# Two macaron layers with routed experts on one core: own slots for every block, and three smaller edits

## The chip, the cores and the metric

One core of a Trainium2 chip runs the kernel. TensorE (PE in the profile) multiplies matrices into PSUM, VectorE (DVE) and ScalarE (ACT) work elementwise and read PSUM, GpSimd (POOL) issues the indirect transfers, and SyncE (SP) issues all others. The time is that of the whole program on the device, in microseconds (us). Every engine runs its own list of instructions in order; they wait for each other only through semaphores.

## The reference, cut to what matters

There are 2048 tokens of width 128. A layer is: half a routed feed-forward, attention, half a routed feed-forward. There are two such layers, so four feed-forward stages (s = 0 to 3), with attention after stage 0 (squared-relu attention over 256 tokens) and after stage 2 (linear attention with a running sum).

```
x = x + 0.5 * L0_ffn(layernorm(x))     # stage 0
x = x + L0_attn(layernorm(x))
x = x + 0.5 * L0_ffn(layernorm(x))     # stage 1
x = x + 0.5 * L1_ffn(layernorm(x))     # stage 2
x = x + L1_attn(layernorm(x))
x = x + 0.5 * L1_ffn(layernorm(x))     # stage 3

# a feed-forward: rms norm, scores = xn @ router.T, the best 2 of 8 experts,
# h = u * silu(gate), y = h @ w_down[e].T, the two y weighted and summed, plus the skip
# linear attention: kv = cumsum_t(K_t outer V_t); out_t = Q_t . kv_t / (Q_t . cumsum(K)_t)
```

## The kernel before

**Tiles and parts.** The tokens form 4 blocks (b0 to b3) of 512. In each stage a block's 1024 (token, expert) pairs are sorted by expert into 15 tiles of 128 rows, each with one expert. The 16 parts (stage s, block b) follow each other: 240 tiles in all, one tile per *slot* t. PE in slot t multiplies tile t with the up and gate weights (`up`, L1045 for layer 0 with 256 hidden units, L1052 for layer 1 with 352), and then tile t-2 with the down weights (`down`, L1006 and L1008), for which DVE must have made u * silu(gate) of that tile (`mult`, L698), which in turn waits for ACT's silu (L593). PE can thus run some two slots ahead of DVE and no further; three PSUM banks hold the up and gate results.

**Rows.** Every four tiles (a round) SP loads 512 sorted rows (L395), PE transposes them into bank S[2] (`rows`, L1067), and ACT copies them (L598). The load of a round stands five slots ahead of its tiles in SP's list, and it waits until all eight scatters of its block have landed; the weights of a tile (L409) stand four slots ahead, in the same list, and so behind such a wait. Round 0 of the first part isn't loaded: DVE makes 0/1 matrices (`onehot`, L871 and L874) and PE sorts the rows by multiplying with them (L1061).

**The side chains.** Beside the tiles each block goes through: gather its y rows from DRAM (POOL, eight indirect transfers, L525), `combine` (DVE, L745), attention after stages 0 and 2 (steps 3 to 21), and `route` for the next stage: `stats` (L702), `guess` (variance and an inverse root of ten dependent small steps, L708 to L726), `norm` (L730), `skip` (L783, and ACT's L610), `z` (PE transposes, L1078), `score` (PE L1083, DVE L793), `first` and `second` (the two best experts), `rank` (PE L1089), `assign` (DVE, L844 to L862, the row numbers), `weights`, and `scatter` (POOL, eight indirect transfers, L504). Where a step stands is read from tables: `ROUTE`, `ATTENTION` and `COMBINE` give the slot of each step, counted from `end_of(s, b)`, which is where the block's part ends (for the first routing it is `LEAD` slots ahead of the block's first part). `WAY` says which row of the tables a block uses; before, nearly all blocks use row 0. Slots ahead of 0 hold no tiles: there the tables set only the order of the steps. A step's slot is a place in every engine's list, not a time; on POOL there is nothing else in the list, so a later slot there means later only where another POOL step comes in between.

**Bank S[2].** `z`, `score`, `rank` and `rows` take turns in it (`S2_TURN`). PE's `claim` waits until all earlier turns have been read: `rows` after a `score` waits for DVE's L793, after a `rank` for DVE's L850. In PE's list a slot goes: up, down, rows, and then the chains' steps, in order of the block's chain.

**POOL in the second attention.** Steps 13 to 16 form the outer products of K and V (L559) on POOL; ACT rounds them (L651) and DVE forms the rest (L895), for the running sums on PE (L1167, L1168).

## Time and profile before

| | |
|---|---|
| runs | 741.56, 747.86, 764.09 us (median 747.86) |
| profiled execution | 741.62 us, span 739.9 us |
| PE busy | 620.9 us (84%), 4590 matmuls |
| DVE busy | 456.0 us (62%) |
| ACT, POOL busy | 264.9 us (36%), 281.8 us (38%) |
| mean granted PE clock | 0.941 of full speed |
| chain that ended last | PE 50%, DVE 26%, issue 9%, DMA 6% |

A share is of the whole span, over stages with different limits. The parts are between 32 and 54 us long: the first matmul of the first tile starts at 34.6 us; parts of stage 0 without and with attention beside them, the parts of stage 1, and so on differ in what runs beside the tiles. Idle time of an engine costs only where it lies on the chain.

### The profile page before, as it was taken

Reading aid. Unit: us, or ns where it says so; the run is one execution under the profiler, and the core shown is the slowest. Engines: PE = TensorE matmul, PEld = TensorE weight load, DVE = VectorE, ACT = ScalarE, POOL = GpSimd, SP = SyncE. Lnnn points to the kernel's source line nnn. Section 1 sums busy time; section 2 is a strip of 40 time slices with the busy share of each in tenths; the row PEclk is TensorE's granted clock in tenths of the full one; section 3 lists DMA queues with packets and bytes.
Section 4 is the critical chain, followed back from the end, with each engine's and each line's share of the span. In section 5 each row is a group of like instructions: output and inputs, shape, how many; then the busy total and the mean of one; then the engine's idle time right before and its main releaser. Section 6 shows DMA issues by size and latency. Waiting matters only on the chain.

```text
span 739.9 us, 15773 instructions
## 1 busy us (share of the span) xinstructions
PE 620.9 (84%) x4590; PEld 567.5 (77%) x4590; DVE 456.0 (62%) x1649; ACT 264.9 (36%) x549; POOL 281.8 (38%) x327
## 2 busy tenths in 40 slices
PE   1688798987969888778888987989979979988977
PEld 1377778777768787777877987978868968877966
DVE  7765545827448257455445664967967969763445
ACT  2134342532514324333323344326326326323221
POOL 2444552160440613563514446044245147052314
PEclk9999999999998999989899999979969989999989
DMA  7388786645545457757656885645645645657752
GB/s 257 102 242 277 220 248 181 181 125 163 163 126 157 125 166 207 229 171 231 204 155 192 246 246 162 170 135 153 189 137 142 196 123 163 203 156 230 236 138 74
DMA packets 113271, 133.59 MB, mean 181 GB/s; under 512 B 10931, under 2 KB 76227, under 8 KB 112806
## 3 DMA queue, kind: packets, MB, share of 16 engines
q1 hardware_dynamic: 104998, 115.79, 53.9%
q0 software_dynamic: 8192, 16.79, 7.6%
q8 instruction: 42, 0.69, 0.4%
q14 instruction: 39, 0.32, 0.1%
HBM read 103.83 MB, written 28.71 MB: 179 GB/s over the span
## 4 chain that ended last, share of the span: by engine, by line
PE 50%; DVE 26%; issue 9%; DMA 6%; another core or an unknown queue 3%; ACT 3%; POOL 2%; POOLq 0%; DVEq 0%; SPq 0%
PE up_gate L1052 13%; PE up_gate L1045 10%; PE y L1006 8%; DVE hidden L698 4%; DVE x_res L745 3%; DMA rows_dram<-rms_out,rows_of 2%; PE side L1067 2%; PE y L1008 2%; PE side L1133 2%; DMA y_rows<-y_dram,rows_of 2%; PE side L1149 2%; PE side L1083 1%; DVE root_square L725 1%; DVE root_square L724 1%
## 5 line engine op out<-in xcount | busy, mean ns | idle before, releaser
L698 DVE TENSOR_TENSOR hidden<-up_gate,hidden 128x256 f32<-128x256 f32 (+1 forms) x240 | 115.5, 489 | 193.7 <-ACT hidden L593 79.1
L504 POOL DMA_INDIRECT rows_dram<-rms_out,rows_of x128 | 129.8, 1014 | 249.7 <-DVE rows_of L855 183.2
L1052 PE MATMUL up_gate<-rows_T,up 128*128 128x128 f32 x1440 | 196.6, 287 | 21.0 <-ACT rows_T L598 8.7
L1052 PEld LDWEIGHTS up_gate<-rows_T,up 128*128 128x128 f32 x1440 | 182.1, 200 | 30.0 <-issue 15.6
L525 POOL DMA_INDIRECT y_rows<-y_dram,rows_of x120 | 121.0, 1008 | 183.5 <-issue 119.3
L593 ACT ACTIVATE hidden<-up_gate 128x256 f32<-128x256 f32 (+1 forms) x240 | 103.9, 436 | 240.8 <-PE up_gate L1045 112.8
L1045 PE MATMUL up_gate<-rows_T,up 128*128 128x128 f32 x960 | 139.5, 291 | 13.4 <-issue 9.0
L1045 PEld LDWEIGHTS up_gate<-rows_T,up 128*128 128x128 f32 x960 | 126.4, 203 | 24.1 <-issue 22.1
L1006 PE MATMUL y<-down,hidden 128*128 x480 | 77.9, 287 | 16.7 <-DVE hidden L698 14.8
L1006 PEld LDWEIGHTS y<-down,hidden 128*128 128x128 f32 x480 | 67.1, 202 | 18.4 <-issue 18.4
L1006 PE MATMUL y<-down_a,hidden 128*128 x480 | 75.9, 282 | 0.0
L598 ACT ACTIVATE rows_T<-side,norm 128x512 f32<-128x512 f32 x64 | 42.3, 661 | 81.0 <-PE side L1067 41.2
L1006 PEld LDWEIGHTS y<-down_a,hidden 128*128 128x128 f32 x480 | 65.9, 199 | 0.0
L586 ACT ACTIVATE y_tile<-y 128x512 f32<-128x512 f32 x64 | 36.5, 570 | 48.9 <-PE y L1008 25.0
L1008 PE MATMUL y<-down_b,hidden 96*128 x240 | 48.0, 282 | 0.0
L1067 PE MATMUL side<-ident,rows 128*128 128x128 f32 x236 | 37.9, 282 | 8.0 <-DVE row_of L850 4.4
L1008 PEld LDWEIGHTS y<-down_b,hidden 96*128 96x128 f32 x240 | 37.9, 198 | 0.1
L1078 PE MATMUL side<-ident,rms_out 128*128 128x128 f32 x64 | 12.4, 326 | 29.4 <-DVE rms_out L730 22.6
L1067 PEld LDWEIGHTS side<-ident,rows 128*128 128x128 f32 x236 | 28.8, 146 | 9.3 <-issue 8.6
L1078 PEld LDWEIGHTS side<-ident,rms_out 128*128 128x128 f32 x64 | 8.5, 165 | 31.0 <-issue 16.2
L610 ACT ACTIVATE x_res<-x_res,b_skip_add,b_skip_mul 128x128 f32<-128x128 f32 x64 | 26.2, 482 | 8.7 <-issue 4.9
L745 DVE SCALAR_TENSOR_TENSOR x_res<-y_rows,w_first,x_res 128x128 f32<-128x128 f32 x64 | 24.1, 418 | 5.4 <-DMA y_rows<-y_early,early_rows_of 3.7
(195 smaller groups left out, 698.3 us busy)
## 6 DMA issues: line engine op xcount, KB each, us to landing
up<-in_up SPq DMA_DIRECT2D x120, 352.0 KB
up<-in_up SPq DMA_DIRECT2D x120, 256.0 KB
rows<-rows_dram SPq DMA_DIRECT2D x47, 256.0 KB
y_dram<-y_tile SPq DMA_DIRECT2D x45, 256.0 KB
rows_dram<-zeros SPq DMA_DIRECT2D x12, 256.0 KB, 3.3
rows<-rows_dram SPq DMA_DIRECT2D x16, 192.0 KB
y_dram<-y_tile SPq DMA_DIRECT2D x15, 192.0 KB
rows_dram<-rms_out,rows_of POOLq DMA_INDIRECT x128
```

The costliest lines, as they stand in the source:

```text
L504: pool.indirect_dma_start(out=xg_d[g], out_offset=bass.IndirectOffsetOnAxis(ap=pos[g][:, at:at + 1], axis=0), in_=xs(Z, GROUPS[g][c // TB] ...
L525: pool.indirect_dma_start(out=gath[b % 2][:, (TB * k2 + c) * P:(TB * k2 + c + 1) * P], out_offset=None, in_=y_d[g], in_offset=bass.Indirec ...
L586: act.activation(ysb[r % 4][:, 0:n * P], Y[r % 2][:, 0:n * P], ACT.Copy).then_inc(y_done, 1)
L593: act.activation(hid[n % 4][:, 0:w], src, ACT.Silu).then_inc(silu_done, 1)
L598: act.activation(xgT[r % 3][:, 0:n * P], S[2][:, 0:n * P], ACT.Copy, scale=wn[:, LAYER[s]:LAYER[s] + 1]).then_inc(s2_free, 1)
L698: dve.tensor_tensor(h, u, h, ALU.mult).then_inc(mult_done, 1)
L745: last = dve.scalar_tensor_tensor(xs(X, b, c * P, P), gath[b % 2][:, (TB * k2 + c) * P:(TB * k2 + c + 1) * P], wk[:, c:c + 1], xs(X, b, c ...
L1006: last = pe.matmul(y, hid[n % 4][:, c * P:(c + 1) * P], w, start=(c == 0), stop=(l == 0 and c == 1))
L1008: last = pe.matmul(y, hid[n % 4][0:96, 2 * P:3 * P], dn1b[:, bass.ds(v * P, P)], start=False, stop=True)
L1045: last = pe.matmul(U[q % 3][:, i * P:(i + 1) * P], upW[n % RING][:, at:at + P], rows_, start=True, stop=True)
L1052: last = pe.matmul(U[q % 3][:, c * P:(c + 1) * P], upW[n % RING][:, at + c * P:at + (c + 1) * P], rows_, start=True, stop=True)
L1067: last = pe.transpose(S[2][:, c * P:(c + 1) * P], xg[r % 4][:, c * P:(c + 1) * P], ident[:, :])
```

## The change

Four edits. (1) Each block gets its own row of the tables (`WAY` becomes 0, 1, 2, 3 in every stage), and nearly all slots move; `LEAD` goes from 38 to 40; `guess` gets a wait for the last block's `skip_ready`, as `skip` may now stand behind it. (2) The outer products of the second attention go from POOL to DVE, at the same steps 13 to 16. (3) The row numbers 1 to 512 (two memsets and a scan) are made at the head of DVE's list, not in the first `score`. (4) `onehot` finishes its matrices one after the other and releases each; PE waits for each. Of the tables only the entries are shown that matter here (both stand for slots after `end_of`):

```diff
-LEAD = 38
+LEAD = 40
 COMBINE, stages 0, 1, 2, 3
-  ((8, 10),), ((11, 16),), ((7, 13),), ((7, 10),)
+  ((7, 8) x4), ((10, 15) x4), ((8, 11), (6, 8), (6, 11), (6, 11)), ((10, 11), (9, 9), (9, 10), (9, 10))
 ATTENTION[0], block 0
-  3: 11, 4: 11, 5: 12, 6: 12, 7: 14, 8: 15, 9: 16, 10: 17, 11: 18, 12: 19, 13: 19, 14: 20, 15: 21
+  3: 8, 4: 11, 5: 11, 6: 12, 7: 15, 8: 16, 9: 16, 10: 16, 11: 17, 12: 17, 13: 18, 14: 18, 15: 19
+  (block 1: steps 12 to 15 all at 18; block 2: 10 to 14 all at 17, 15 at 18)
 ATTENTION[2], blocks 0 and 1
-  3: 13, 4: 14, 5: 15, 6: 16, 7: 17, ... 13: 22, 14: 22, 15: 23, 16: 24, ... 20: 29, 21: 30
+  3: 11, 4: 14, 5: 15, 6: 15, 7: 17, ... 13: 21, 14: 23, 15: 24, 16: 25, ... 20: 29, 21: 30
+  3: 13, 4: 14, 5: 15, 6: 15, 7: 17, ... 13: 21, 14: 21, 15: 24, 16: 25, ... 20: 29, 21: 30
 ROUTE[0], blocks 0, 1, 2, 3 (before: rows 1, 2, 0, 0)
-  b0 stats 8, guess 10, root 11, norm 16, skip 17, z 20, score 23, first 23, second 23, rank 24, assign 24, weights 27, scatter 30
-  b1 stats 5, guess 7, root 8, norm 8, skip 13, z 13, score 18, first 18, second 18, rank 23, assign 23, weights 26, scatter 24
-  b2, b3 stats 3, guess 3, root 8, norm 8, skip 15, z 9, score 12, first 12, second 15, rank 17, assign 17, weights 25, scatter 23
+  b0 stats 4, guess 15, norm 18, skip 18, z 19, score 20, first 23, second 24, rank 24, assign 27, weights 33, scatter 41
+  b1 stats 3, guess 8, norm 9, skip 17, z 10, score 15, first 17, second 18, rank 25, assign 25, weights 29, scatter 33
+  b2 stats 1, guess 5, norm 7, skip 18, z 8, score 10, first 16, second 16, rank 16, assign 17, weights 25, scatter 32
+  b3 stats 1, guess 5, norm 7, skip 18, z 8, score 10, first 15, second 15, rank 15, assign 16, weights 24, scatter 31
 ROUTE[1]
-  stats 21, guess 21, norm 23, skip 31, z 26, score 27, first 28, second 28, rank 30, assign 30, weights 30, scatter 30
+  stats 19, guess 20, norm 21, skip 28, z 23, score 24, first 24, second 27, rank 29, assign 29, weights 33, scatter 29
 ROUTE[2]
-  stats 16, guess 17, norm 20, skip 31, z 22, score 23, first 24, second 25, rank 27, assign 27, weights 36, scatter 29
+  stats 15, guess 16, norm 18, skip 23, z 19, score 20, first 22, second 24, rank 26, assign 26, weights 38, scatter 29
 ROUTE[3]
-  stats 30, guess 30, norm 30, skip 37, z 32, score 32, first 32, second 32, rank 34, assign 34, weights 35, scatter 37
+  stats 31, guess 31, norm 31, skip 41, z 33, score 34, first 34, second 34, rank 35, assign 35, weights 37, scatter 41
-WAY = ((1, 2, 0, 0), (0, 0, 0, 0), ...)
+WAY = ((0, 1, 2, 3), (0, 1, 2, 3), ...)
```

```diff
 # guess
+                    after(dve, skip_ready, k - 1)
 # first score
-                        dve.memset(R[5], 1.0)
-                        link(dve.memset(R[4], 1.0))
-                        link(dve.tensor_tensor_scan(R[4], R[5], R[4], 0.0, ALU.mult, ALU.add))
 # onehot
-                    last = dve.tensor_scalar(R[c], R[4], rows_1[:, 2 * c:2 * c + 1], None, ALU.is_equal)
-                link(last)
-                for c in range(TB):
-                    last = dve.scalar_tensor_tensor(R[c], R[4], rows_1[:, 2 * c + 1:2 * c + 2], R[c], ALU.is_equal, ALU.add)
-                last.then_inc(onehot_ready, 1)
+                    link(dve.tensor_scalar(R[c], R[4], rows_1[:, 2 * c:2 * c + 1], None, ALU.is_equal))
+                    dve.scalar_tensor_tensor(R[c], R[4], rows_1[:, 2 * c + 1:2 * c + 2], R[c], ALU.is_equal, ALU.add).then_inc(onehot_ready, 1)
 # attention, taken out of POOL's list and put into DVE's
+                if l == 1 and j in (13, 14, 15, 16):
+                    ...
+                    dve.tensor_tensor(R[3 + t].rearrange("p (h f g) -> p h f g", f=F, g=G),
+                                      kk.unsqueeze(3).to_broadcast([P, HEADS, F, G]),
+                                      vv.unsqueeze(2).to_broadcast([P, HEADS, F, G]), ALU.mult).then_inc(kv_ready, 1)
 # ahead of DVE's first slot
+            dve.memset(R[5], 1.0)
+            link(dve.memset(R[4], 1.0))
+            link(dve.tensor_tensor_scan(R[4], R[5], R[4], 0.0, ALU.mult, ALU.add))
 # PE, rows of round 0
-                    pe.wait_ge(onehot_ready, 1)
                     claim("rows", r)
                     for c in range(TB):
+                        pe.wait_ge(onehot_ready, c + 1)
                         last = pe.matmul(S[2][:, :], xs(Z, 0, c * P, P), R[c], start=(c == 0), stop=(c == TB - 1))
```

## Rows read from the trace of the kernel before

**Rows 1.** Busy time by stretch: us, then each engine's busy us, PE clock, DMA share.

```profile
99.00:139.70 40.70, 37.54 (x268) 32.98 (x268) 22.58 (x90) 16.05 (x33) 10.11 (x11) 1.00 0.72 209
139.70:186.90 47.20, 41.34 (x274) 36.37 (x274) 26.13 (x110) 17.77 (x38) 15.93 (x16) 0.93 0.51 148
...
478.60:533.00 54.40, 49.27 (x346) 44.28 (x345) 43.40 (x129) 21.51 (x42) 20.96 (x20) 0.87 0.54 156
...
587.30:640.00 52.70, 46.47 (x346) 42.59 (x346) 44.60 (x134) 21.29 (x42) 21.40 (x20) 0.94 0.57 165
```

**Rows 2.** Timeline of the start: start us, us long, engine, line, what, [idle before <-releaser].

```profile
9.77 0.38 DVE L708 BATCH_NORM_AGGREGATE b_meanvar<-b_stats 128x2 f32<-128x6 f32 x4
...
12.59 0.17 DVE L726 SCALAR_TENSOR_TENSOR b_rstd<-root_square,b_rstd 128x8 f32<-128x8 f32 x1
...
15.25 0.19 DVE L793 COPY scores<-side 128x32 f32<-128x32 f32 x1
...
26.57 0.18 DVE L793 COPY scores<-side 128x32 f32<-128x32 f32 x1
...
26.90 5.96 PE L1061 MATMUL side<-attention,rms_out 128*128 128x512 f32 x8 [2.83 <-DVE attention L874]
...
34.55 1.15 PE L1045 MATMUL up_gate<-rows_T,up 128*128 128x128 f32 x8 [1.69 <-issue]
```

**Rows 3.** Timeline: the third block's first transposes, and the first scatters' end.

```profile
31.86 0.97 POOL L504 DMA_INDIRECT rows_dram<-rms_out,rows_of  x1 [0.30 <-issue]
...
34.17 0.38 SPq L395 DMA_DIRECT2D rows<-rows_dram  x1
...
40.19 0.66 PE L1078 MATMUL side<-ident,rms_out 128*128 128x128 f32 x4 [3.38 <-DVE rms_out L730]
```

**Rows 4.** Timeline of POOL: first and last gather of b0, last gather of b1.

```profile
76.05 1.04 POOL L525 DMA_INDIRECT y_rows<-y_dram,rows_of  x1 [4.00 <-DMA rows_dram<-rms_out,rows_of]
...
86.57 0.99 POOL L525 DMA_INDIRECT y_rows<-y_dram,rows_of  x1 [0.33 <-issue]
...
120.17 1.00 POOL L525 DMA_INDIRECT y_rows<-y_dram,rows_of  x1 [0.30 <-issue]
```

**Rows 5.** Timeline of PE: the first transposes of the third and fourth parts' rows.

```profile
94.61 0.60 PE L1067 MATMUL side<-ident,rows 128*128 128x128 f32 x4
...
136.85 0.63 PE L1067 MATMUL side<-ident,rows 128*128 128x128 f32 x4 [1.10 <-DVE scores L793]
```

**Rows 6.** Chain of waits, 660 to 690 us: start us, us, what was waited for.

```profile
673.78 5.27 DMA rows_dram<-rms_out,rows_of
...
679.10 3.03 DMA rows<-rows_dram
```

**Rows 7.** Timeline: a down matmul beside the stage-1 routing.

```profile
173.38 0.71 PE L1006 MATMUL y<-down,hidden 128*128 x4 [2.70 <-DVE hidden L698]
```

**Rows 8.** Timeline at the last routing of the second block.

```profile
539.11 0.87 DVE L702 BATCH_NORM_STATS2 b_stats<-x_res 128x6 f32<-128x128 f32 x4
...
544.22 1.11 PE L1078 MATMUL side<-ident,rms_out 128*128 128x128 f32 x4 [2.97 <-DVE rms_out L730]
```

**Rows 9.** Busy time in stretches of 2 us, columns as in rows 1.

```profile
544.00:546.00 2.00, 1.11 (x4) 0.71 (x4) 2.00 (x7) 0.63 (x1) 1.70 (x2) 0.50 0.65 219
...
556.00:558.00 2.00, 2.00 (x10) 1.73 (x11) 0.38 (x1) 0.19 (x1) 0.00 (x0) 0.71 0.03 8
```

**Rows 10.** Timeline beside POOL's outer products.

```profile
509.93 2.27 DVE L888 TENSOR_SCALAR w_first<-w_sum 128x4 f32<-128x4 f32 x1
...
510.05 2.12 POOL L559 TENSOR_TENSOR attention<-attention 128x512 f32<-128x512 f32 x2
...
513.51 0.68 DVE L895 TENSOR_TENSOR kv_lo<-attention,kv_hi 128x512 fp32r<-128x512 f32 x1
...
513.65 1.39 POOL L504 DMA_INDIRECT rows_dram<-rms_out,rows_of  x1 [0.30 <-issue]
...
514.12 2.19 DVE L745 SCALAR_TENSOR_TENSOR x_res<-y_rows,w_first,x_res 128x128 f32<-128x128 f32 x2
```

More of the change, by code:

```diff
@@ L64 @@
 DOWN = 2
+TURN = 1
 ROWS_AT = 2
 LOAD_ROWS = 3
[L67 to L74 removed]
+LEAD = 40
+LAG = (0, 0, 0, 0, 0)
+COMBINE = (((7, 8), (7, 8), (7, 8), (7, 8),),
[3 rows of a table added]
+ATTENTION = (({3: 8, 4: 11, 5: 11, 6: 12, 7: 15, 8: 16, 9: 16, 10: 16, 11: 17, 12: 17, 13: 18, 14: 18, 15: 19},
[3 rows of a table added]
              None,
[L76 removed]
[4 rows of a table added]
@@ L77 @@
              None)
-ROUTE = (({"stats": 3, "guess": 3, "root": 8, "norm": 8, "skip": 15, "z": 9, "score": 12, "first": 12, "second": 15, "rank": 17, "assign": 17, "weights": 25, "scatter": 23},
-          {"stats": 8, "guess": 10, "root": 11, "norm": 16, "skip": 17, "z": 20, "score": 23, "first": 23, "second": 23, "rank": 24, "assign": 24, "weights": 27, "scatter": 30},
-          {"stats": 5, "guess": 7, "root": 8, "norm": 8, "skip": 13, "z": 13, "score": 18, "first": 18, "second": 18, "rank": 23, "assign": 23, "weights": 26, "scatter": 24},),
-         ({"stats": 21, "guess": 21, "root": 23, "norm": 23, "skip": 31, "z": 26, "score": 27, "first": 28, "second": 28, "rank": 30, "assign": 30, "weights": 30, "scatter": 30},),
-         ({"stats": 16, "guess": 17, "root": 17, "norm": 20, "skip": 31, "z": 22, "score": 23, "first": 24, "second": 25, "rank": 27, "assign": 27, "weights": 36, "scatter": 29},),
-         ({"stats": 30, "guess": 30, "root": 30, "norm": 30, "skip": 37, "z": 32, "score": 32, "first": 32, "second": 32, "rank": 34, "assign": 34, "weights": 35, "scatter": 37},))
@@ L84 @@
-WAY = ((1, 2, 0, 0), (0, 0, 0, 0), (0, 0, 0, 0), (0, 0, 0, 0), (0, 0, 0, 0))
+ROUTE = (({"stats": 4, "guess": 15, "norm": 18, "skip": 18, "z": 19, "score": 20, "first": 23, "second": 24, "rank": 24, "assign": 27, "weights": 33, "scatter": 41},
+          {"stats": 3, "guess": 8, "norm": 9, "skip": 17, "z": 10, "score": 15, "first": 17, "second": 18, "rank": 25, "assign": 25, "weights": 29, "scatter": 33},
+          {"stats": 1, "guess": 5, "norm": 7, "skip": 18, "z": 8, "score": 10, "first": 16, "second": 16, "rank": 16, "assign": 17, "weights": 25, "scatter": 32},
+          {"stats": 1, "guess": 5, "norm": 7, "skip": 18, "z": 8, "score": 10, "first": 15, "second": 15, "rank": 15, "assign": 16, "weights": 24, "scatter": 31},),
+         ({"stats": 19, "guess": 20, "norm": 21, "skip": 28, "z": 23, "score": 24, "first": 24, "second": 27, "rank": 29, "assign": 29, "weights": 33, "scatter": 29},
+          {"stats": 18, "guess": 19, "norm": 21, "skip": 28, "z": 23, "score": 24, "first": 24, "second": 27, "rank": 29, "assign": 29, "weights": 35, "scatter": 29},
+          {"stats": 18, "guess": 19, "norm": 21, "skip": 28, "z": 23, "score": 24, "first": 24, "second": 27, "rank": 29, "assign": 29, "weights": 35, "scatter": 29},
+          {"stats": 18, "guess": 19, "norm": 21, "skip": 28, "z": 23, "score": 24, "first": 24, "second": 25, "rank": 27, "assign": 27, "weights": 33, "scatter": 27},),
+         ({"stats": 15, "guess": 16, "norm": 18, "skip": 23, "z": 19, "score": 20, "first": 22, "second": 24, "rank": 26, "assign": 26, "weights": 38, "scatter": 29},
+          {"stats": 15, "guess": 16, "norm": 18, "skip": 23, "z": 19, "score": 20, "first": 22, "second": 24, "rank": 26, "assign": 26, "weights": 38, "scatter": 29},
+          {"stats": 15, "guess": 16, "norm": 18, "skip": 23, "z": 19, "score": 20, "first": 22, "second": 24, "rank": 26, "assign": 26, "weights": 38, "scatter": 29},
+          {"stats": 15, "guess": 16, "norm": 18, "skip": 23, "z": 19, "score": 20, "first": 23, "second": 25, "rank": 26, "assign": 26, "weights": 37, "scatter": 28},),
+         ({"stats": 31, "guess": 31, "norm": 31, "skip": 41, "z": 33, "score": 34, "first": 34, "second": 34, "rank": 35, "assign": 35, "weights": 37, "scatter": 41},
+          {"stats": 31, "guess": 31, "norm": 31, "skip": 41, "z": 33, "score": 34, "first": 34, "second": 34, "rank": 35, "assign": 35, "weights": 37, "scatter": 41},
+          {"stats": 31, "guess": 31, "norm": 31, "skip": 41, "z": 33, "score": 34, "first": 34, "second": 34, "rank": 35, "assign": 35, "weights": 37, "scatter": 41},
+          {"stats": 31, "guess": 31, "norm": 31, "skip": 41, "z": 33, "score": 34, "first": 34, "second": 34, "rank": 35, "assign": 35, "weights": 35, "scatter": 41},))
@@ L85 @@
+WAY = ((0, 1, 2, 3), (0, 1, 2, 3), (0, 1, 2, 3), (0, 1, 2, 3), (0, 1, 2, 3))
 SPAN = 60
-FIRST_SLOT = -30
+FIRST_SLOT = -60
 END_SLOT = SLOTS + 14
```

29 lines of the change are left out of this document (7 added, 22 removed), and 10 rows, old and new, of tables (ATTENTION, COMBINE).

## The prediction

> **What bounds the kernel now.** I read first the busy times by part, then the PE timeline for every gap of over half a microsecond, then the timelines of the other engines around each such gap. The parts show two kinds of loss. The stretch of the third part and that of the fourth hold the same kind of work (a part of tiles and one attention, 268 and 274 matmuls), but take 40.7 and 47.2 us [rows 1]: the fourth loses 6.5 us to waits and to a clock of 0.93. Two more stretches like the fourth follow (48.2 and 45.8 us in the same view). In the second attention the stretch of 54.4 us has DVE busy for 43.4 us and PE for 49.3 us at a clock of 0.87, that is 42.9 us at full clock [rows 1]; there are two such and a third of 52.7 us. There neither engine is full: they stop each other. So order, not work, is what a schedule can win here, and an idle engine is only the symptom: what counts is whose list stands still.
>
> **The start.** The row numbers are made while the chip waits for x, so the first scores needn't be copied at 15.25 but some 2.5 us earlier, as DVE's small steps before them ended at 12.76 [rows 2]. But the second block's guess, which filled that wait (9.77 to 12.76, 3.0 us), now stands between the first block's `first` and `second`, so it goes on the path: 3.0 - 2.5 = 0.5 us later. The release of matrices one by one is worth nothing: the first sorting matmul must also claim bank S[2], the second block's scores are the turn before, and DVE copies them only behind the whole one-hot. PE started at 26.90, just behind that copy at 26.57 and not behind a matrix [rows 2]; the list keeps this order. Bounds: 0, and 3 us if the claim weren't there. I take 0. Then the third block's transposes, z, which stood behind two tiles and waited 3.4 us [rows 3], now stand ahead of the first tile, with its scores behind the first; what is lost is that two tiles no longer fill the wait: two tiles of 1.15 us [rows 2], 2.3 us, less the score step of about 1 us that doesn't come later. Start in all: 0.5 + 1.3, about +2 us (bounds 0 and +4).
>
> **First routing, blocks b2 and b3.** `first`, `second` and `rank` now share a slot, and the row load's turn follows `assign` by none or three slots, so PE waits for some 2 us of small DVE steps twice; before, one such wait of similar size was there. +1 us (bounds 0 and +4), but for b3 it hides under the next item.
>
> **POOL's order.** This is the one thing the new table makes worse. The scatter of b2 moves from slot 15 to slot 22, behind the gathers of b0 (slots 18 to 21). POOL's list holds nothing else, so before it scattered early; now it can't start until the eighth gather has been issued: 86.57 + 0.99 + 0.30 = 87.9 us [rows 4]. Eight scatters at 0.97 + 0.30 = 1.27 us [rows 3]: the last starts at 96.8. From there SP's row load was issued 2.3 us later at the start [rows 3], and a row load took 3.0 us, in a loaded stretch 5.3 and 3.0 [rows 6]. So the rows are there at 102.1 to 105.1, and PE wants them at 94.61 [rows 5]: a stop of 7.5 to 10.5 us; I take 9. Behind the waiting row load stand SP's weight loads from tile 30 on and a y store; they go out back to back once it is free. The same swap at b3 (slot 30 to 36) goes behind seven eighths of b1's gathers: last gather 120.17, scatters until 130.4, rows at 138.7 by the loaded lags against 136.85 [rows 4 to 6]: 2 us, and up to 5 if PE comes earlier. Sum +11.
>
> **First attention and stage-1 routing.** The x update, stats and guess stood in one slot and held back the next product on DVE by 4.6 us, so `down` waited 2.7 us [rows 7]. Stats and guess now have a slot each, norm comes later, skip (ACT) leaves the attention's steps, and steps 8 to 15 stand together, so that PE runs through them while ACT and DVE follow. No work goes. Ceiling: the three long stretches down to 40.7: 6.5 + 7.5 + 5.1 = 19.1 us [rows 1]. The combine now stands only one slot after its first half, at +8 instead of +10, where the last gathers land: DVE waits there 2 to 3 us, about what PE's lead covers. I take three quarters, -15 (bounds -19 and 0).
>
> **Stages 1 to 2.** All steps move up by a slot or two; `rank` gains a slot on the row load's claim. The z step has one slot instead of two behind norm. -4 (bounds -8 and +3).
>
> **Second attention and last routing.** Before, stats, guess and norm ran from 539.11 for 5.1 us in slot 30 and PE stood 3.0 us at z two slots on [rows 8], and the clock was at half from 544 until 557 [rows 9]: 13 us at 1.2 GHz, worth 6.5. Now the x update and the other block's normalise are in slot 30, the chain in slot 31, z in slot 33 and score in 34: by the durations PE reaches z just as norm is done. After it PE waits about 1 us for `second`, as rank follows one slot after. Floor: the DVE time of 43.4 plus 4 to 5 us of waits, 48; ceiling of the gain 6.5 + 6.5 + 4.5 = 17.5 us. I take -15 (bounds -17.5 and 0). For the last block the gain is none: there the row load waits for POOL's gathers and scatters, not for z [rows 6].
>
> **Outer products.** DVE gets 16 of 0.68 us (the row of the same shape [rows 10]), +10.9 us. It loses what POOL's cost it: `w_first`, a step of 0.15 to 0.35 us, took 2.27 us until POOL's two were done, and the first combine 2.19 instead of 0.6 [rows 10]; 2.1 + 1.6 in each of three blocks, -11.1 us. Sum 0 (bounds -4 and +6). POOL's scatters lose four products from their midst. A scatter's issue beside a DVE step with two SBUF inputs took 1.39 us instead of 1.0 [rows 10]. The Trainium skill ("SBUF — State Buffer", "SBUF: two separate sides") says the shared port pair is an exclusive lock and that a blocked GpSimd delays the descriptors of its transfers; by it each outer product would hold a scatter for its whole 0.68 us, against 0.4 in the row, some 11 us of POOL's time instead of 6. Neither is on the path, as POOL is busy for only 21 of 54 us.
>
> **Sum.** Start +2, first routing +1, POOL's order +11, some 2 us of half clock behind its stops (taken from [rows 9], where 3 us of idling were followed by 13 at half clock, but here the matmuls behind are fewer), attentions -15 and -15, stages between -4, products 0: -18 us. The profiled execution took 741.6 us (span 739.9), so 723.6. The median of the runs shown lies 6.3 us above it, and the runs spread from 741.6 to 764.1; I take half of that offset: **727 us**.
>
> **Rivals.** (a) *The waits really go.* With the ceilings (-19, -4, -17.5) and POOL's order at 7.5 + 2, the sum is 2 + 1 + 9.5 + 2 - 40.5 = -26, and 719 us; with the stages between at -8 and the start at 0, 713. For it: PE's own work is 42.9 us in stretches of 54 [rows 1]. Against: every hop from PE to DVE is a wait, and both engines are near full there. Chance 0.2. (b) *DVE is the bound of the second attention.* Its list now has the products too, and a combine, three steps and stats meet in slot 41 (176, 191); if the 44 us of DVE work [rows 1] keep their waits, -15 becomes 0 and the products cost 3: 727 + 18 = 745 us. For it: 43.4 of 54.4 us busy [rows 1]. Against: the wait at z is DVE's list in one slot, and just that is split. Chance 0.26. (c) *Slower: POOL's order.* The same mechanism at its upper bounds: b2's rows at 105.1 instead of 94.61, 10.5 us; b3's 5; each stop long enough to drop the clock, 6.5 us for each [rows 9]; 28.5 instead of my 13. It decides if it goes together with (b): 745 + 15.5 = 760.5, and 764 with the whole offset of the median. The point from which it makes the kernel slower than the runs shown is a stop of some 15 us with nothing gained in the second attention. Chance 0.12. That the release of matrices does nothing is in the sum already.
>
> **Chances and range.** The forecast's own case (718 to 736) has 0.42. This kernel's measurement can tell some 2% from no change: 732.9 and 762.8 us. Faster: 0.2 of (a) and most of the forecast, 0.37; same: its rest and (b), 0.31; slower 0.12. For 8 in 10 the range runs from 708, inside (a), to 750, over (b); (c) is left out.
>
> **What would show it.** Right: the last scatter of b2 is issued after b0's gathers and PE has a gap of 7 to 11 us ahead of the row transposes of the third part; PE's sorting matmul starts right behind the copy of the second block's scores; the fourth to sixth parts take 41 to 43 us; no gap over 2 us ahead of z at the last routing, no stretch of 13 us at half clock there, stretches of 49 to 51 us with DVE at 43; `w_first` at 0.2 us everywhere. Wrong: the second attention's stretches still at 54 us (then (b)), or the third part's gap missing, which would take 11 us more off.

## The result and the profile after

The changed kernel takes 754.8 us (median of 20 runs, 745.2 to 765.9), the kernel before in the same runs 747.8 us (740.4 to 764.1). The recorded ratio is **1.019 (95% 1.013 to 1.026)**, where 727 us were predicted; the two medians alone give 1.009. Slower either way, but not clearly by 2%. The profiled execution took 751.6 us (span 749.9), against 741.6 us (739.9) before.

The first reading is the busy time by stretch, now over the whole span. Columns as in [rows 1]; the seven stretches are the start, the first two parts of 15 tiles, the third, the fourth to sixth, the seventh to tenth, the eleventh to fourteenth (second attention), and the rest. First the kernel before:

```profile
0.00:34.60 34.60, 12.23 (x38) 7.61 (x38) 26.80 (x128) 7.33 (x16) 12.52 (x63) 1.00 0.56 183
34.60:99.00 64.40, 52.33 (x426) 48.74 (x426) 38.64 (x165) 24.60 (x59) 29.96 (x30) 0.97 0.81 241
...
139.70:280.90 141.20, 122.71 (x816) 108.04 (x816) 74.23 (x305) 53.07 (x111) 47.85 (x48) 0.93 0.51 147
280.90:431.60 150.70, 127.84 (x1030) 122.45 (x1031) 81.87 (x348) 53.16 (x117) 65.41 (x66) 0.94 0.71 208
431.60:640.00 208.40, 185.56 (x1357) 168.95 (x1355) 161.39 (x466) 83.78 (x162) 82.29 (x79) 0.92 0.58 163
640.00:739.90 99.90, 82.70 (x662) 78.72 (x662) 50.48 (x152) 26.93 (x54) 33.62 (x32) 0.94 0.60 171
```

(the third part's 40.70 us stand in [rows 1]), and then the changed kernel:

```profile
0.00:37.00 37.00, 13.41 (x42) 8.18 (x42) 28.29 (x132) 7.43 (x17) 12.64 (x63) 0.99 0.55 178
37.00:116.60 79.60, 58.22 (x417) 55.46 (x418) 37.84 (x161) 24.91 (x58) 24.02 (x24) 0.84 0.60 183
116.60:160.60 44.00, 39.42 (x274) 33.72 (x274) 24.27 (x99) 16.04 (x32) 16.02 (x16) 0.98 0.68 202
160.60:296.10 135.50, 121.79 (x819) 104.84 (x819) 75.32 (x310) 53.72 (x113) 49.00 (x49) 0.95 0.53 156
296.10:451.40 155.30, 127.12 (x1025) 123.34 (x1025) 81.03 (x339) 53.83 (x120) 66.40 (x67) 0.92 0.70 204
451.40:652.20 200.80, 177.37 (x1357) 160.56 (x1355) 154.04 (x476) 83.16 (x159) 61.76 (x61) 0.98 0.60 167
652.20:749.90 97.70, 81.67 (x662) 78.57 (x662) 50.44 (x152) 26.91 (x54) 33.14 (x32) 0.95 0.61 178
```

The stretches differ by +2.4, +15.2, +3.3, -5.7, +4.6, -7.6 and -2.2 us, in sum +10.0. The losses at the front were predicted in kind (20.9 us against 16); the gains behind come to 10.9 us instead of 34, and one stretch has the wrong sign.

The announced signs came out as follows. The scatter of b2 stands behind b0's gathers, and PE stops for 6.84 us ahead of the third part's row transposes (before it stood still for nothing there, [rows 5]); POOL, SP and PE in the timeline of the changed kernel:

```profile
98.13 1.02 POOL L521 DMA_INDIRECT rows_dram<-rms_out,rows_of  x1 [1.18 <-issue]
...
107.81 0.97 POOL L521 DMA_INDIRECT rows_dram<-rms_out,rows_of  x1 [0.30 <-issue]
...
110.10 0.38 SPq L412 DMA_DIRECT2D rows<-rows_dram  x1
...
113.14 1.12 PE L1077 MATMUL side<-ident,rows 128*128 128x128 f32 x4 [6.84 <-DMA rows<-rows_dram]
```

The first scores are copied at 12.88 instead of 15.25, and the sorting matmul still starts right behind the second block's scores, released one by one or not. `w_first` takes 0.27 us, where it took 2.27 [rows 10]. PE's wait at z fell from 2.97 us for the second block [rows 8] to 0.34 (the first block's is in the lines below, 0.82), and waits at rank came in its place, of 2.33, 0.91, 1.44 and 1.48 us for the four blocks. One announced sign did not come: the fourth to sixth parts were to take 41 to 43 us each and took 43.8, 46.4 and 45.4. The lines:

```profile
12.88 0.19 DVE L792 COPY scores<-side 128x32 f32<-128x32 f32 x1 [3.16 <-PE side L1093]
...
27.40 0.18 DVE L792 COPY scores<-side 128x32 f32<-128x32 f32 x1
...
27.64 2.93 PE L1071 MATMUL side<-attention,rms_out 128*128 128x512 f32 x3 [2.91 <-DVE scores L792]
...
507.67 0.66 PE L1088 MATMUL side<-ident,rms_out 128*128 128x128 f32 x4 [0.82 <-DVE rms_out L731]
...
518.33 0.19 PE L1099 MATMUL side<-chosen,before_b 128*128 128x40 bf16 x1 [2.33 <-DVE chosen L807]
...
527.79 0.27 DVE L884 TENSOR_SCALAR w_first<-w_sum 128x4 f32<-128x4 f32 x1
```

What had not been expected stands in the chain of waits. Its share of "another core or an unknown queue" was 3.3% before and is 6.5% now; some of its longest pieces:

```profile
46.83 4.15 another core or an unknown queue
...
223.19 7.73 another core or an unknown queue
...
269.17 5.39 another core or an unknown queue
```

The pieces of over 1 us are 13 with 46 us, against six with 25 us before. The profile names nothing in the kernel that they wait for. They are not times in which the whole core rests: in the piece of 6.34 us at 209.81 in the kernel before, DVE stands for 6.36 us and ACT for 3.85, while PE goes on until 216.6 and POOL goes on issuing gathers. I call them **stops** and asked first whether they belong to the kernel.

### The profile page after: what moved, and what is told of

Its sections match the earlier page's. It is cut to its first block, busy times and chain, and to the rows that moved or that the text cites. A ratio compares the mean times of both kernels' runs of the same rounds, so it can differ in the third digit from the quotient of the medians.

```text
span 749.9 us, 15794 instructions
## 1 busy us (share of the span) xinstructions
PE 619.0 (83%) x4590; PEld 564.7 (75%) x4590; DVE 451.2 (60%) x1665; ACT 266.0 (35%) x549; POOL 263.0 (35%) x311
## 4 chain that ended last, share of the span: by engine, by line
PE 49%; DVE 25%; issue 9%; another core or an unknown queue 6%; DMA 4%; ACT 4%; POOL 1%; DVEq 0%; POOLq 0%; SPq 0%; ACTq 0%
PE up_gate L1062 13%; PE up_gate L1055 11%; PE y L1016 8%; DVE hidden L699 4%; PE side L1093 2%; PE side L1077 2%; DVE attn_xT L954 2%; DMA rows_dram<-rms_out,rows_of 2%; PE y L1018 2%; DVE x_res L746 1%; PE side L1143 1%; ACT hidden L594 1%; PE side L1088 1%; DVE attention L950 1%
## 5 line engine op out<-in xcount | busy, mean ns | idle before, releaser
L1055 PEld LDWEIGHTS up_gate<-rows_T,up 128*128 128x128 f32 x960 | 132.1, 212 | 36.6 <-issue 26.3
L1016 PE MATMUL y<-down,hidden 128*128 x480 | 80.5, 293 | 9.6 <-DVE hidden L699 6.4
L1016 PEld LDWEIGHTS y<-down,hidden 128*128 128x128 f32 x480 | 68.9, 207 | 12.3 <-issue 12.2
L606 ACT ACTIVATE z_T<-side,norm 128x512 f32<-128x512 f32 x16 | 11.0, 687 | 30.6 <-PE side L1088 26.5
```

The lines of the kernel that those rows point to most:

```text
L1016: last = pe.matmul(y, hid[n % 4][:, c * P:(c + 1) * P], w, start=(c == 0), stop=(l == 0 and c == 1))
L1055: last = pe.matmul(U[q % 3][:, i * P:(i + 1) * P], upW[n % RING][:, at:at + P], rows_, start=True, stop=True)
```

## The experiments

All ratios are to the kernel before, run beside them on the same chip.

**1. The first routing's slots as before.**

```
 changed kernel, with
-LEAD = 40
+LEAD = 38
-ROUTE[0]: four rows of the change
+ROUTE[0]: the rows of the kernel before
```

> The changed kernel with one table put back: every slot of the first routing (and the lead of 38 slots) as before; all attention, combine and later routing slots as changed. Theory A (the loss is at the front: in the two profiles the start, the first three parts and the scatters behind the gathers cost 2.4 + 7.0 + 8.2 + 3.3 = 21 us more, some of it paid back by the fourth part's 3.3): the first four parts shrink by 15 to 20 us, the time is 735 to 741 us, ratio to the kernel before 0.98 to 0.99, and no stop ahead of the row transposes of the third part. Rival B (the loss is in unattributed waits, 46 us on the chain of waits of the changed kernel against 24 us before, which come from the way the attention's steps are bunched): the front gets 7 to 10 us shorter at most, the time stays at 745 to 750 us, and the chain still has more than 40 us of unattributed waits.

Measured: 675.0 us (6 runs), ratio 0.972 (0.966 to 0.978).

**2. The two scatters alone.**

```
-ROUTE[0], b2: "scatter": 32   b3: "scatter": 31
+ROUTE[0], b2: "scatter": 25   b3: "scatter": 25
```

> The changed kernel with two numbers changed: the scatters of the third and fourth block start 7 and 6 slots earlier (slots 15 and 30), ahead of the gathers of the first and second block on POOL's list. Theory A: the stop of 6.8 us ahead of the row transposes of the third part goes, the second and third parts get 6 to 11 us shorter, time 744 to 749 us. Rival B (the row load was late for another reason, or PE's stop only moves to the combine behind the gathers): under 3 us shorter, 752 to 755 us.

Measured: 678.3 us, ratio 0.976 (0.970 to 0.981). The second part takes 32.6 us and the third 41.2 us, against 40.8 and 42.4 us of the changed kernel on such a chip (run 5), and PE comes to the transposes without a wait:

```profile
103.28 0.60 PE L1077 MATMUL side<-ident,rows 128*128 128x128 f32 x4
```

**3. The outer products back on POOL**, all slots as changed.

```
-                (DVE) dve.tensor_tensor(R[3 + t]..., ALU.mult).then_inc(kv_ready, 1)
+                (POOL) pool.tensor_tensor(R[3 + t]..., ALU.mult).then_inc(kv_ready, 1)
```

> The changed kernel with the outer products of the second attention back on POOL. Theory A (as in the prediction: 10.9 us of products taken by DVE against 11.1 us of waits for the shared port): the same time within 3 us, 752 to 758 us; w_first shows 2.3 us beside the products again. Rival B (DVE bounds the second attention's stretches, so the products cost it their whole time): 744 to 748 us, the three stretches 2 to 3 us shorter each. Rival C (POOL's products held DVE longer than the rows said): 760 us or more.

Measured: 692.0 us, ratio 0.998 (0.994 to 1.001).

**4. The small edits alone**, on the kernel before: the row numbers ahead of everything, the sorting matrices released one by one, as in the diff of the change; no slot touched.

> The kernel before with two small edits of the change alone: the row numbers made ahead of everything on DVE, and the sorting matrices released one by one. No slot is changed. Theory A: the scores of the first block are copied up to 2.5 us earlier and the start shrinks by 1 to 2.5 us, the release gives nothing, time 745 to 747 us. Rival B (the guess that stands ahead of the scores takes the time): start within 0.5 us, ratio 1.00. It is also a near copy of the kernel before: if its unattributed waits stand at other places than in the profile of the kernel before, they are not made by the order of work.

Measured: 692.7 us, ratio 1.000 (0.997 to 1.004). The start took 33.5 us, against 34.6 in the profile before and 34.0, 34.7 and 33.6 in three other kernels with its start (runs 6, 7 and 16), so no gain stands out. Theory A's time was wrong, its view of the release right.

These four share a chip, and it told more than any of them: the kernel before takes **694 us** there, not 748, and in none of the four profiles has the chain one unattributed piece. The next four ran on a second such chip (695.5 us).

**5. The changed kernel again.**

> The changed kernel itself, unchanged, beside the others. The four kernels measured so far ran on a chip on which the kernel before took 694 us and no chain of waits held an unattributed wait; so the two profiles that the prediction and its result rest on (24 and 46 us of unattributed waits on their chains) held something that does not belong to either kernel. Theory A (those waits are no part of the order of work): where the kernel before takes 694 us again, this takes 690 to 696 us, ratio 0.995 to 1.003, its second and third parts are 7 to 9 us longer than those of the kernel before, its second attention 8 to 10 us shorter, and its fourth to sixth parts are within 1 us of the kernel before. Rival B (the unattributed waits follow from the bunched steps): the ratio is 1.01 to 1.03 again and the chain holds 40 us of them.

Measured: 688.7 us, ratio **0.991 (0.986 to 0.995)**. The stretches of the near copy of the kernel before (run 4, on the other such chip), and of this run:

```profile
0.00:33.50 33.50, 12.39 (x37) 7.59 (x37) 27.21 (x128) 7.33 (x16) 12.73 (x63) 1.00 0.57 189
33.50:99.60 66.10, 54.26 (x425) 50.55 (x425) 39.00 (x165) 24.89 (x58) 29.95 (x31) 0.94 0.80 243
99.60:141.60 42.00, 38.89 (x270) 34.31 (x268) 22.65 (x90) 16.46 (x33) 9.95 (x10) 0.97 0.63 190
141.60:263.00 121.40, 112.43 (x816) 99.19 (x816) 74.68 (x303) 53.44 (x111) 48.38 (x48) 1.00 0.58 170
263.00:394.90 131.90, 121.35 (x1029) 117.65 (x1030) 82.57 (x350) 54.46 (x117) 65.36 (x66) 0.97 0.80 238
394.90:598.00 203.10, 182.10 (x1356) 167.29 (x1354) 161.68 (x466) 84.61 (x162) 81.83 (x79) 0.93 0.58 168
598.00:689.40 91.40, 78.28 (x662) 76.07 (x662) 50.60 (x152) 27.37 (x54) 32.40 (x32) 0.96 0.65 187
```

```profile
0.00:37.10 37.10, 12.52 (x42) 7.88 (x42) 28.41 (x132) 7.73 (x17) 12.86 (x63) 1.00 0.54 177
37.10:111.60 74.50, 57.49 (x418) 54.82 (x419) 37.48 (x161) 24.60 (x58) 24.05 (x24) 0.85 0.64 196
111.60:154.00 42.40, 39.60 (x275) 33.91 (x274) 23.87 (x96) 16.26 (x32) 16.10 (x16) 0.98 0.68 203
154.00:274.80 120.80, 115.02 (x820) 99.25 (x820) 76.19 (x313) 54.39 (x113) 48.67 (x49) 1.00 0.60 177
274.80:403.50 128.70, 119.85 (x1024) 115.67 (x1025) 81.18 (x340) 54.96 (x120) 66.34 (x67) 0.99 0.83 246
403.50:593.90 190.40, 173.34 (x1357) 158.89 (x1355) 153.69 (x476) 83.78 (x158) 61.12 (x61) 0.99 0.62 177
593.90:687.30 93.40, 81.64 (x662) 78.85 (x662) 50.43 (x151) 26.99 (x53) 33.83 (x32) 0.94 0.64 183
```

The differences are +3.6, +8.4, +0.4, **-0.6**, -3.2, **-12.7** and +2.0 us, in sum -2.1 (the medians give -6.5). The fourth to sixth parts of the kernel before take 121.4 us here and took 141.2 us in the profile that the prediction was made from, at almost the same busy times of DVE, ACT and POOL.

**6. First attention alone**: the kernel before with `COMBINE[0]`, `ATTENTION[0]` and `ROUTE[1]` of the change.

> The kernel before with the changed slots of the first combine, the first attention and the second routing alone. Theory A: the prediction's 15 us were read out of stretches of 47 us that were long through unattributed waits; with stretches of 41 us before, these slots give 1 to 3 us (161.8 against 163.3 us for the four parts), and the combine one slot after its first half makes DVE wait for the last gathers ahead of the fourth block's assign, which costs 3 to 5 us in the second part: ratio 0.998 to 1.006. Rival B (the prediction's own): 12 to 15 us less, ratio 0.978 to 0.983.

Measured: 694.3 us, ratio 0.997 (0.993 to 1.002). The 15 us of the prediction are not there. The third to sixth parts take 162.0 us against 163.4 in run 4, and the stop at the second part came as foretold (36.9 us, PE waiting 7.9).

**7. Second attention alone**: the kernel before with `COMBINE[2]`, `COMBINE[3]`, `ATTENTION[2]` and `ROUTE[3]` of the change, products on POOL.

> The kernel before with the changed slots of the third and fourth combine, the second attention and the last routing alone; the outer products stay on POOL. Theory A: the waits at z (2.9 us in each of three blocks) and the clock they cost go, 8 to 12 us less, ratio 0.983 to 0.989. Rival B (the prediction's, with the products): 15 us less, ratio 0.978. Rival C (the z wait only moves to rank and the transposes): under 3 us less, ratio 0.996 or more.

Measured: 683.9 us (four runs, 681.0 to 689.8), ratio 0.984 (0.979 to 0.989): 11 us, theory A. Its profiled execution is the slowest of the four, and in it the four parts of the second attention take 202.8 us against 203.1 in run 4: the slots with the z waits (167, 182, 197) are shorter by 5.9, 7.1 and 6.9 us, but others are longer. So the 11 us rest on the runs' times alone.

**8. Run 1 with the first block's combine spread.**

```
-COMBINE[0], b0: (7, 8)     ATTENTION[0], b0: {3: 8, ...
+COMBINE[0], b0: (8, 10)    ATTENTION[0], b0: {3: 11, ...
```

> The changed kernel with the first routing's slots as before (as in the run that took 675 us) and with the first block's combine at 8 and 10 slots instead of 7 and 8, as before, its attention's first step at 11. In the run of 675 us DVE waited 4.0 us for the last gathers in the second half of that combine and PE stood 6.8 us ahead of the row transposes of the second part, which the assign on DVE behind the combine had to release. Theory A: that stop goes, 4 to 5 us less than 675 us, ratio 0.964 to 0.968. Rival B (the wait moves to the attention, which now starts three slots later): the same time, ratio 0.972.

Measured: 674.8 us, ratio 0.972 (0.966 to 0.978): no difference to run 1, rival B. In run 1 DVE and PE had shown

```profile
89.27 0.61 DVE L746 SCALAR_TENSOR_TENSOR x_res<-y_rows,w_first,x_res 128x128 f32<-128x128 f32 x2 [4.04 <-DMA y_rows<-y_dram,rows_of]
...
93.00 0.88 PE L1077 MATMUL side<-ident,rows 128*128 128x128 f32 x3 [6.81 <-DVE row_of L849]
```

and that stop went (the second part 32.5 us instead of 36.6), but the third part grew from 41.3 to 42.9 us and the fifteenth from 45.4 to 48.5.

**9 and 10. The changed kernel and run 3's kernel, on a chip with stops.** Here the kernel before took 755.8 us.

> The changed kernel unchanged, once more, to stand beside the next kernel on one chip. Theory A (the unattributed waits belong to the chip and not to the kernel): where the kernel before takes 694 us, this takes 0.986 to 0.995 of it; where the kernel before takes 748 us again, the ratio is above 1.0, and both profiles hold a dozen or more stops of 3 to 8 us that stand at other slots than in the first two. Rival B: the stops stand in the same slots of the changed kernel as in its first profile (slots 3, 51, 66, 81, 93, 97, 108, 112, 190, 239).

> The changed kernel with the outer products back on POOL, as in the run of 691.95 us, now on the same chip as the changed kernel itself. Theory A (the prediction's balance, 10.9 us of products against 11.1 us of waits at the shared port): the two kernels within 0.3% of each other. Rival B (the move gives something: the first run stood at 0.9976, the changed kernel on another chip at 0.9908): 0.4 to 0.8% slower than the changed kernel. Rival C (DVE bounds the stretches): 0.4% or more faster than the changed kernel.

Measured: 764.3 us, ratio 1.014 (0.999 to 1.028), and 762.3 us, ratio 1.007 (1.001 to 1.013). So on this chip too the changed kernel shows no gain, though its interval takes in 1.0. Rival B of run 9 held in part: four of the ten named slots, 66, 81, 93 and 108, are long again. The slot from one tile's first up/gate matmul to the next one's is in slot 66, 81, 93 and 108 longer than on the chip without stops by 3.9, 2.5, 6.0 and 5.9 us in the first profile of the changed kernel and by 3.9, 2.9, 6.3 and 4.9 us in this one; run 10 has 4.6, 1.6, 6.2 and 5.6. The busy time around slot 93 of run 9, by the microsecond, and its timelines of PE and ACT:

```profile
302.00:303.00 1.00, 0.41 (x4) 0.21 (x2) 0.00 (x0) 0.00 (x0) 0.52 (x1) 1.00 0.45 168
303.00:304.00 1.00, 0.47 (x2) 0.30 (x2) 0.00 (x0) 0.00 (x0) 0.97 (x1) 1.00 0.22 78
304.00:305.00 1.00, 0.21 (x1) 0.19 (x1) 0.00 (x0) 0.16 (x1) 0.18 (x1) 1.00 0.19 66
305.00:306.00 1.00, 0.17 (x2) 0.12 (x2) 0.68 (x5) 0.64 (x2) 0.79 (x1) 1.00 0.00 0
```

```profile
301.69 0.72 PE L1055 MATMUL up_gate<-rows_T,up 128*128 128x128 f32 x5
303.33 0.47 PE L1055 MATMUL up_gate<-rows_T,up 128*128 128x128 f32 x2 [0.92 <-issue]
304.79 0.27 PE L1055 MATMUL up_gate<-rows_T,up 128*128 128x128 f32 x1 [0.98 <-issue]
...
304.84 0.38 ACT L594 ACTIVATE hidden<-up_gate 128x256 f32<-128x256 f32 x1 [5.54 <-remote]
```

The eight matmuls of one group, with no semaphore between them, start up to 1.3 us apart, while the transfers fall to nothing: by the trace neither a semaphore nor a transfer holds PE here.

**11 and 12. The first routing undone, on a third chip** (the kernel before: 740.4 us, with stops), the second with the first block's steps 4 to 6 at 12, 12 and 13 as well.

> The changed kernel with the first routing's slots and lead as before, once more, to stand on one chip with the two others. Theory A: 0.970 to 0.975 on a chip that takes 694 us for the kernel before, 0.975 to 0.985 on one that takes 748 us or more. Rival B (on such a chip a denser order of work is stopped more often): 0.99 or more there.

> The changed kernel with the first routing's slots and lead as before, and the first block's combine at 8 and 10; its attention's first steps at 11, 12, 12 and 13 (stats and guess in slots of their own, where in the run of 674.76 us they shared a slot and PE waited 2.2 us at down). Theory A: 1 to 3 us less than the kernel with the first routing alone undone, ratio to the kernel before 0.965 to 0.972 on a chip without unattributed waits. Rival B: no difference between the two. On a chip that takes 748 us or more for the kernel before: theory A (the stops are about as many in every kernel) 15 to 20 us faster than the kernel before, ratio 0.975 to 0.985; rival B (a denser order of work has more of them) ratio 0.99 or more.

Measured: 729.9 us, ratio 0.986 (0.980 to 0.992), and 730.4 us, ratio 0.984 (0.972 to 0.997). A gain remains, half of that on the chips without stops (0.972 in runs 1 and 8), and just at the upper end of theory A.

**13. More instructions on SP.**

```
+for _ in range(3):
+    sp.value_load(eid[g][0:1, a:a + 1], min_val=0, max_val=E - 1)
 v = sp.value_load(eid[g][0:1, a:a + 1], min_val=0, max_val=E - 1)
```

> The changed kernel with three more reads of the tile's expert number into a register ahead of each weight load on SP, whose values are not used: some ten more instructions a tile on an engine that is otherwise idle. In the profiles with unattributed waits the stops stand in slots in which the kernel issues 24 to 34 instructions a microsecond, against 26 in the mean, and two in three of them above 28. Theory A (the stops have to do with the number of instructions that all engines issue together): on a chip with stops the time grows by 15 us or more, on a chip without them by less than 3 us. Rival B (the stops belong to a place in the order of the data transfers or to one engine): no difference to the changed kernel on either.

Measured: 901.7 us, ratio 1.230, and it says nothing of the stops: SP's queue has 34% of the chain. Such a read keeps an engine's sequencer for 0.6 us (PE's own in the trace of run 9 goes from 300.28 to 300.87), three of them 1.8 us of a slot of 2.9, and I had not counted that.

**14 and 15. The changed kernel, and cheaper instructions beside it**, on the chip of runs 11 and 12 (the kernel before: 740.8 us).

```
+for _ in range(12):
+    sp.wait_ge(bias_loaded, 16)
```

> The changed kernel unchanged, as the measure for the next run on the same chip. Where the kernel before takes about 695 us: 0.991 (both theories). Where it takes 740 us or more: 1.013 to 1.02, and its stops of 3 us and more stand in slots 66, 81, 93, 108 and 127 again, as in its two profiles with stops (theory A: they belong to places in the order of work) or elsewhere (rival B: they come by chance).

> The changed kernel with twelve more waits a tile on SP, each on a count that was reached long before, ahead of the weight load. In the run with three more register reads (901.7 us) each read took 0.65 us of SP, and SP itself became the bound; these waits should take 0.05 us each, 0.6 us of the 2.9 us of a slot. Theory A (the stops have to do with the number of instructions that all engines issue together, here some 4 a microsecond more on 26): no difference on a chip without stops, 10 us or more above the changed kernel on a chip with stops. Rival B (they have not): within 3 us of the changed kernel on either.

Measured: the changed kernel 739.0 us (four runs between 723.8 and 754.0, which give no ratio; the medians give 0.998), its slots 66 and 81 again longer by 3.9 and 2.6 us, 93 and 108 not; with the waits 757.2 us, ratio 1.025 (1.015 to 1.034), 18 us more by the medians. Half of the waits are no instructions of their own in the trace, which holds 1410 more, of 0.03 to 0.05 us each. The unattributed share of the chain was 4.3% without and 8.3% with them.

**16. The slots between the attentions alone** (`COMBINE[1]`, `ROUTE[2]`), same chip.

> The kernel before with the changed slots between the attentions alone: the combine at 10 and 15 slots and the third routing. Theory A: the waits ahead of the row transposes of the seventh and eighth part (4.2 us in the seventh) go, the parts 1.2 to 2.1 together get 2 to 4 us shorter (128.8 against 131.9 us in the two kernels' profiles without stops), ratio 0.994 to 0.998. Rival B (as in the first profile pair, where the same four parts came out 4.5 us longer): ratio 1.004 or more.

Measured: 740.9 us, ratio 1.004 (0.999 to 1.009): unclear. The stretches of [rows 1] answer here, with the same slots as in the kernel before:

```profile
98.30:140.80 42.50, 39.34 (x269) 34.52 (x269) 23.16 (x91) 16.71 (x34) 9.04 (x10) 0.96 0.65 192
140.80:189.50 48.70, 40.08 (x273) 34.42 (x273) 25.86 (x109) 17.39 (x37) 16.69 (x16) 0.96 0.50 143
189.50:236.40 46.90, 40.74 (x275) 35.89 (x274) 26.48 (x110) 17.66 (x37) 16.27 (x16) 0.93 0.52 150
```

The fourth part takes 48.7 us on this chip and 41.0 us in run 4. The slots that lengthen it and the next two are those of the kernel before in its own profile: slots 48, 69 and 78 are 2.9, 3.3 and 2.6 us longer there than in run 4, and 2.3, 2.0 and 2.2 us here.

**17 and 18. The last two on a chip without stops** (the kernel before: 694.2 us).

> The changed kernel with the additional satisfied waits on SP, once more. On a chip with stops it took 757.2 us against 739.0 us of the changed kernel (1410 more instructions of 0.045 us). On a chip where the kernel before takes about 695 us, theory A (the stops grow with the instructions issued; the waits themselves are free) says within 3 us of 0.991 of the kernel before, 686 to 692 us; rival B (SP's later weight loads cost the 18 us) says 700 us or more there. On a chip with stops both say 1.02 again.

> The changed kernel with the first routing's slots as before and the first block's combine and stats spread, which took 0.984 of the kernel before on a chip with stops. Theory A (its gain is the first routing's and the second attention's, and the stops dilute it): 0.965 to 0.972 where the kernel before takes about 695 us, 0.978 to 0.988 where it takes 740 us or more. Rival B (the spread of the first block's steps costs what it saves): 0.973 or more on a chip without stops.

Measured: with the waits 691.7 us, ratio 0.999 (0.995 to 1.003), inside the 686 to 692 us of theory A; 3 us (by the ratios 0.8%) above the changed kernel on another such chip, against 18 on one with stops. And **669.8 us, ratio 0.968 (0.963 to 0.974)**: the changed kernel with the first routing's slots as before and the first block's combine and statistics spread is the fastest here, by 0.4% of the kernel before against run 1, with intervals that overlap. Against the kernel before it gains on both kinds of chip; against the changed kernel it is clear without stops only.

## Why the prediction was wrong

The sum was -18 us against the kernel before. The profiles give +10.0 on the first chip and -2.1 without stops. Step by step:

- **Start, +2: right.** +2.4 and +3.6. The release of matrices one by one gave nothing, as costed.
- **First routing +1, POOL's order +11, half clock +2: the place was right, the size not.** The three parts cost +18.5 us on the first chip and +8.8 without stops, against 14. The announced stop ahead of the third part was 6.84 us, where I took 9. Two numbers in the table, the scatters, account for most of it: 688.7 against 678.3 us, 1.5% of the time, in runs 5 and 2 (two chips without stops). The row load left SP 2.3 us behind the last scatter's issue and landed 3 us later, as in [rows 3, 6]. What the first part lost (+7.0 in the first profile) is mostly a stop: 0.8 us in run 5.
- **First attention and stage-1 routing, -15: wrong, and this is the step that failed.** It took the ceiling from the difference between a stretch of 40.7 us and three of 47.2, 48.2 and 45.8 us in one execution [rows 1], and put it down to waits and to the clock that this order of work makes. The same order takes 41.0, 41.1 and 39.2 us in run 4, and 48.7 and 46.9 in run 16. So the 6 to 7 us belong to the execution and not to this order of work, and so does the clock of 0.93 (1.00 in run 4). In the chain of waits of the kernel before they look like this, and after each of them the clock is at half for 3.4 to 6.8 us:

```profile
152.17 1.95 issue
...
209.81 6.34 another core or an unknown queue
...
247.53 1.90 issue
```

Only the one of 6.34 us is given to nothing by name; in the other two parts the same kind of wait (ACT stands for 3.24 us with the releaser "remote" ahead of 151.37) reaches the chain as "issue". What the slots are worth is -0.6 us in run 5 and 0.3% of the time in run 6, whose interval takes in no gain as well. The down matmul's wait of 2.7 us [rows 7] was real, but it lies in a stretch in which PE is busy for 112.43 of 121.40 us (run 4), so that there were 9 us to win at all, not 19.
- **Stages between, -4: -3.2 without stops**, +4.6 in the first profile, whose chain has six unattributed pieces of over 1 us in this stretch against two before. By itself it was not shown: run 16 is unclear.
- **Second attention and last routing, -15: right in kind, a quarter too large.** -12.7 and +2.0 behind it in run 5, 11 us in run 7 alone. The z wait went, and the clock of the stretch is 0.99 instead of 0.93. Without stops PE's waits at z and rank together fell only from 9.8 us (run 4) to 7.0 us (run 5) over the four blocks, so most of the gain lies elsewhere, in the clock above all: PE's busy time fell from 182.10 to 173.34 us for the same matmuls. The waits at rank took back 0.9 us a block without stops, as said (1 us), and up to 2.3 us on the first chip.
- **Outer products, 0: right.** Runs 3 and 5 stand at 0.998 and 0.991 on two chips, runs 10 and 9 the other way on one, 762.3 and 764.3 us; the four parts of the second attention take 191.6 us with POOL's products and 190.4 with DVE's (runs 3 and 5). The trace of the changed kernel also shows how a scatter fares beside a product:

```profile
522.05 1.03 POOL L521 DMA_INDIRECT rows_dram<-rms_out,rows_of  x1 [5.24 <-DVE rows_of L854]
...
522.68 1.28 DVE L896 TENSOR_TENSOR attention<-attention 128x512 f32<-128x512 f32 x2
...
523.38 1.46 POOL L521 DMA_INDIRECT rows_dram<-rms_out,rows_of  x1 [0.30 <-issue]
```

Five scatters of this profile began inside a product. They took 1.46, 1.46, 1.00, 1.36 and 1.46 us instead of 1.0, in sum 1.7 us of POOL's time. The Trainium skill ("SBUF — State Buffer", "SBUF: two separate sides") lets the later of the two wait for the whole rest of the earlier, where a DVE step with two SBUF inputs meets a GpSimd op that reads SBUF. By it the scatter at 523.38 would have been 0.6 us longer, as the second product ran until 523.96; it was 0.46 us longer. Two more that were 0.46 us longer began only 0.01 us ahead of a product's end, but beside the next DVE step of the same kind (L902, 0.69 us), so these rows don't tell which step held them. A price of 0 to 0.5 us a scatter is what they give.

With the first attention at -0.6 the prediction's own sum is -3.6 us, and the runs without stops gave -2.1 in the profile and -6.5 in the medians. That this is near is in part luck, as the loss at the front was 5 us smaller and the gain of the second attention 2 to 4 us smaller than forecast. That leaves 12 to 14 us by which the changed kernel loses more than the kernel before in the first pair. On the other two chips with stops it is less certain: 1.014 has an interval from 0.999, and 0.998 stands on four scattered runs, against 0.991 without stops. Where the first pair's loss is can be seen in part: in unattributed pieces of the chain, 46 us against 25. The run with twelve more waits supports that they grow with the number of instructions that all engines issue together (18 us there, 3 without stops), but the 3 us compare two chips, and the 18 us lean on four runs that spread over 30. If it is so, an order of work in which the engines stand closer has more of them; that was not shown.

What makes the stops is **open**: the profile puts no semaphore and no transfer of the kernel behind them, they come in part at the same places in three profiles of the changed kernel and in a kernel that differs from it by one step, and on three chips they don't come at all. Loading of the program itself is an obvious rival, and the traces speak against it: its two queues move 42 and 39 packets in the changed kernel with stops and without, none of them longer than 2 us, and none starts between 213.4 and 232.3 us, where the longest stop of the first profile lies (223.19 to 230.92). Work of other cores of the chip, and the writing of the profile's own records, which would also grow with the number of instructions, were not tested.

Rival (b), which was to be seen by stretches still at 54 us, did not happen (50.4, 52.8 and 52.7 us; 48.9, 48.5 and 50.2 in run 5); rival (c)'s mechanism did, at 9 to 10 us (runs 5 and 4, runs 5 and 2) instead of 28.5.

## What to carry to other kernels

A ceiling read from two stretches of one execution is only as good as the reason for their difference: look first whether the longer one holds waits that the profile gives to nothing, and take the same stretch from a second execution, if possible on another chip, before a term of the sum is built on it. The second is the surer test: here only 6.34 of some 20 us bore that label. In a table of slots the order on the queue with one list (POOL's scatters behind its gathers) can weigh more than the steps around it: of what undoing the first routing gave, two numbers account for 1.5% (0.991 to 0.976) and all its other entries for 0.4% (0.972). Of a change in many parts, undo the part that the trace shows to lose; the rest was worth 3%.

## What the runs showed of the hardware

- The kernel before took 694 to 695.5 us on three chips, 740 and 756 us on two others, and 748 us in the first pair. On the slower ones the chain of each profile of these kernels holds three to eleven unattributed pieces of 3 to 8 us, in which DVE and ACT stand while PE and POOL may go on; on the three fast chips it holds none in ten profiles. The granted clock is lower with them (0.94 to 0.96 in the changed kernel's profiles, 0.97 without stops), and a result of 1% changed its sign: 0.991 without stops, 1.019 in the first pair.
- In one stop (slot 93 of run 9) matmuls of one group start up to 1.3 us apart, where they follow by 0.11 us, and for 1 us no transfer is under way. In others transfers go on.
- A read of a value into a register keeps the sequencer for 0.6 us, a wait that is long satisfied for 0.03 to 0.05 us.
